# Turning softmax probabilities by four full-array turns a head instead of sixteen quarter-array ones

## The reference

```python
q = (inputs_q @ Wq).reshape(b, sq, H, HD) * (1.0 / np.sqrt(HD))
k = (inputs_kv @ Wk).reshape(b, skv, H, HD)
v = (inputs_kv @ Wv).reshape(b, skv, H, HD)
scores = jnp.einsum('bqhd,bkhd->bhqk', q, k)
attn = jax.nn.softmax(scores, axis=-1)
ctx = jnp.einsum('bhqk,bkhd->bqhd', attn, v).reshape(b, sq, H * HD)
return ctx @ Wo
```

## Time and profile before

| | |
|---|---|
| runs of the kernel before | 1133.2, 1135.2, 1136.26 us |
| median | 1135.2 us |
| profiled execution, from first to last instruction | 1132.8 us |
| TensorE busy in it | 1032.7 us (91%) |
| mean granted TensorE clock in it | 0.950 |
| stage with the change | about 232.5 to 512 us of the span |

### The profile page before, as it was taken

One profiled execution on the slowest core, in us unless ns is written; L12 is line 12 of the kernel. 1 busy time (PEld: TensorE's weight loads), 2 busy tenths in 40 slices (PEclk: granted clock), 3 DMA queues, 4 the chain that ended last, 5 costly groups with the idle time before them and its releaser, 6 DMA issues.

```text
span 1132.8 us, 17516 instructions
## 1 busy us (share of the span) xinstructions
PE 1032.7 (91%) x6658; PEld 691.2 (61%) x6658; DVE 565.9 (50%) x1286; ACT 367.3 (32%) x687; POOL 265.6 (23%) x336
## 2 busy tenths in 40 slices
PE   5979999989999999988865799999959999997989
PEld 4766699446767676757645577777723434453467
DVE  5876423534434343446466221221257787657792
ACT  3562233232121212213311121221204566735660
POOL 5421431500000000003431222222152453302350
PEclk9995999999999999999895999999976999998999
DMA  9003032211011010057017102111010400020000
GB/s 290 25 2 103 19 97 86 84 43 29 22 31 38 25 38 5 11 197 262 1 33 283 33 28 72 69 33 42 14 66 19 157 1 1 2 75 1 0 6 33
DMA packets 37432, 67.25 MB, mean 59 GB/s; under 512 B 4456, under 2 KB 27080, under 8 KB 35816
## 3 DMA queue, kind: packets, MB, share of 16 engines
q1 hardware_dynamic: 29960, 51.98, 13.5%
q0 software_dynamic: 4080, 11.15, 3.5%
q10 hardware_dynamic: 3312, 3.02, 0.8%
HBM read 54.72 MB, written 11.40 MB: 58 GB/s over the span
## 4 chain that ended last, share of the span: by engine, by line
PE 76%; DVE 12%; ACT 5%; DMA 3%; issue 2%; POOL 2%; SPq 0%; DVEq 0%; ACTq 0%; POOLq 0%
PE bank L354 22%; PE bank L1269 12%; PE bank L1293 7%; PE bank L1619 6%; PE bank L2340 5%; PE bank L2365 3%; PE bank L2386 3%; PE bank L1629 3%; PE bank L1282 2%; PE bank L1604 2%; PE bank L2835 2%; PE bank L1594 2%; PE bank L2404 1%; DVE big L2622 1%; DMA big<-yg,big 1%
## 5 line engine op out<-in xcount | busy, mean ns | idle before, releaser
L1269 PE MATMUL bank<-big 128*128 x552 | 147.7, 418 | 0.6 <-ACT big L1154 0.6
L354 PE MATMUL bank<-XNT,big 128*128 128x512 f32 x296 | 137.9, 615 | 7.1 <-DVE big L2575 5.6
L1269 PEld LDWEIGHTS bank<-big 128*128 128x128 f32 x552 | 98.3, 192 | 39.2 <-issue 2.5
L270 POOL TENSOR_TENSOR rstd<-ve,half 128x1 f32<-128x1 f32 x48 | 27.8, 584 | 330.5 <-DVE ve L264 330.2
L2340 PE MATMUL bank<-big,xs 32*128 32x512 f32 x256 | 89.9, 739 | 11.6 <-DVE xs L281 10.1
L354 PEld LDWEIGHTS bank<-XNT,big 128*128 128x128 f32 x296 | 55.8, 196 | 70.8 <-issue 59.9
L2195 DVE TENSOR_REDUCE big<-bank 128x2 f32<-128x512 f32 x128 | 82.0, 685 | 21.1 <-PE bank L2340 20.4
L1293 PE MATMUL bank<-big 128*128 (+1 forms) x368 | 87.2, 380 | 1.1 <-ACT big L1169 1.1
L1047 DVE TENSOR_TENSOR big<-big,bank 128x704 f32<-128x704 f32 x23 | 20.4, 889 | 124.6 <-ACT big L1162 124.6
L2286 ACT ACTIVATE big<-bank 128x1024 f32<-128x1024 f32 x64 | 64.9, 1024 | 40.2 <-PE bank L2365 39.9
L354 PE MATMUL bank<-CTXT,big 128*128 128x512 f32 (+1 forms) x192 | 67.0, 494 | 11.0 <-DMA big<-wvT 11.0
(11 more groups left out here) (350 smaller groups left out, 1803.2 us busy)
## 6 DMA issues: line engine op xcount, KB each, us to landing
big<-m_gu SPq DMA_DIRECT2D x8, 1408.0 KB
big<-m_d SPq DMA_DIRECT2D x8, 768.0 KB
big<-a_qk SPq DMA_DIRECT2D x16, 256.0 KB, 2.9
yg<-big ACTq DMA_DIRECT2D x23, 128.0 KB, 2.1
big<-m_gu SPq DMA_DIRECT2D x8, 352.0 KB
big<-a_o SPq DMA_DIRECT2D x16, 128.0 KB, 2.0
xn<-XNT SPq DMA_DIRECT2D x8, 256.0 KB, 6.0
big<-f_keys SPq DMA_DIRECT2D x1, 2048.0 KB, 9.2
```

The lines of the kernel that those rows point to most:

```text
L270: e.tensor_tensor(k.rstd[at % NT][:, :], k.ve[at % NT][:, :], k.half[:, 0:1], ALU.pow).then_inc(k.ln_rstd, 1)
L354: ins = e.matmul(out, a, b, start=start and n == 0, stop=stop and n == len(pairs) - 1)
L1269: ins = e.matmul(out, xgT[s % 2][:, kb, :], WB[:, bass.ds(at[s] + (kb * 2 * F + c * chunk), chunk)], start=kb == 0, stop=kb == KB - 1)
```

## The change

Two things change, both on TensorE. `turn_p` now issues four turns, each of the full 128 partitions by 128 columns, that is two tiles with both halves. Such a turn moves the block of tile 2i + j and half b to the partitions of half j and the columns of tile 2i + b: half and tile parity change places. So that `pv` still finds each sequence where it looks, `scores` puts another sequence into each block: n = 4(t // 2) + 2b + t % 2 in place of 2t + b. The number and shapes of the matmuls in `scores` stay.

```diff
             for t in range(NT):
                 for b in (0, 1):
-                    c = slice((2 * t + b) * SEQ, (2 * t + b + 1) * SEQ)
+                    n = 4 * (t // 2) + 2 * b + t % 2
+                    c = slice(n * SEQ, (n + 1) * SEQ)
                     ins = e.matmul(bank[b * SEQ:(b + 1) * SEQ, SB_, t * SEQ:(t + 1) * SEQ], qT[h % 2][:, c],
                                    kT[h % FIRST][:, c], start=True, stop=True)
             ins.then_inc(S["s_ps"], 1)
...
             if h > 0:
                 e.wait_ge(S["pt_dve"], h)
-            for t in range(NT):
-                for b in (0, 1):
-                    ins = e.matmul(bank[rows(b), TB, t * SEQ:(t + 1) * SEQ], pb[rows(b), t], k.ident[rows(b), rows(b)],
-                                   start=True, stop=True)
+            for i in range(NT // 2):
+                ins = e.transpose(bank[:, TB, i * P:(i + 1) * P], pb[:, 2 * i:2 * i + 2].rearrange("p t m -> p (t m)"),
+                                  k.ident[:, :])
             ins.then_inc(S["pt_ps"], 1)
```

## The result

| | before | after |
|---|---|---|
| median of the runs | 1134.45 us (4 runs) | 1123.0 us (4 runs, 1122.22 to 1125.54) |
| ratio | | 0.9906, 95% interval 0.9886 to 0.9927 |
| profiled execution, span | 1132.8 us | 1123.8 us (its own time 1125.54) |
| mean granted clock | 0.950 | 0.947 |
| the stage, scores(0) to the start of the last output projection | 269.3 us | 257.9 us |

The changed kernel is faster by 0.7 to 1.1%. The forecast was 1123.3 us. Run again later with six executions, it gave 1122.5 us and a ratio of 0.9907 (0.9885 to 0.9929).

What follows compares the result with a forecast made beforehand. TensorE alone was taken to bound the stage; 0.83 us saved in each of heads 2 to 13, plus heads 0, 1, 14 and 15, made 11.9 us, so 1135.2 - 11.9 = 1123.3 us, range near 1120.3 to 1128.

Steps and rivals of the forecast that it cites:

- What bounds the stage: From 246 to 494 us TensorE alone bounds, busy for 247.76 of 248.00 us, with much room on all other engines.
- The price of the old turn: In a usual head, 1.27 us of TensorE's time: 1.07 for 32 records plus 0.10 lost at each edge.
- the first rival: Turns cost 0.11 us but the edges stay, not made by tiling; 9.4 us saved, 1125.8 us; chance 0.20.
- The price of the new turn: Four full-array turns at 0.11 us each, 0.44 us with no edge cost; a usual head saves 0.83 us.
- The rival of 0.27 each: New turns don't overlap; a usual head saves 0.19 us, 2.3 us in all, 1132.9 us; chance 0.06.
- the slower rival: Turns don't keep the clock up, so it falls mid-stage; 1150 us with one low stretch per head; chance 0.04.
- What is late next: Turned-probabilities copy delays nothing; the output projection's middle pause stays; head 14 loses 0.3 us waiting for ACT's copy.
- The sum: Savings over heads 0 to 15, 11.9 us together, 9.96 of it from heads 2 to 13.
- From the span to the median: Median of the runs taken as 2.4 us above the profiled span, carried over: 1135.2 - 11.9 = 1123.3 us.

Runs made afterwards that it cites:

- quarter pair: Changed kernel with one pair of the old 64 x 64 matmuls added behind the four transposes; 1129.82 us, ratio 0.9966 to the kernel before.
- halves apart: Kernel before with the turn's sixteen 64 x 64 matmuls reordered, eight of the upper half, then eight of the lower; 1147.98 us, ratio 1.0124.
- early projection: In head 15 alone, head 14's output projection goes ahead of the turn; on the changed kernel 1119.25 us (0.9876), on the kernel before 1130.29 us (0.9971).

## Why the prediction was right

- *What bounds the stage.* Right: TensorE alone. What its queue lost, the stage lost; heads 2 to 13 each gave 0.83 or 0.84 us.
- *The price of the old turn, 1.27 us with its edges.* The sum is right, its split is not: 1.08 and 0.10 at each edge is what the starts of the groups show, but 0.14 of the 1.08 are seams as well, so that the sixteen small matmuls are 0.94 and the seams 0.33. Since the new turn removes all of it, the error cancels. The edges vanish with plain full-array matmuls at the same wait, and come back with one quarter pair; in the quarter pair, 0.23 us of its 0.34 are there for the change of tiling, and a short full-array matmul has the rest too. This was the difference between the forecast and the first rival (1125.8), and it is the step that the Trainium skill ("TensorEngine Tiling (Array Packing)", Key Properties) had spoken for; the runs agree that changing the tiling costs time.
- *The price of the new turn, 0.44 us.* Right: 0.437, and 0.109 for each turn added. The rival of 0.27 each took a record's length for its price. The full clock held from 250 to 480 us, so that the slower rival had no case in the usual heads; 0.44 us of turns in 17.68 is all that this shows of it. One argument against that rival was weak: that the clock line shows no low slice around the full-array turns before head 0. A slice of that line is 28 us. The trace before has a stretch of 3.4 us at half clock just behind the second eight of those turns, where TensorE had idle times of 1.46 and 0.78 us too, so that it says nothing on turns either way:

```profile
232.20:235.60 3.40, 3.08 (x4) 1.51 (x5) 0.00 (x0) 0.22 (x1) 0.00 (x0) 0.50 0.00 0
```

- *What is late next.* Right in all three: the copy starts 0.20 us after the projection does, the first addition at 1.14, and head 14 lost 0.3 us to ACT's copy.
- *The sum.* Forecast 11.9 us; the stage gained 11.4. By heads, forecast and measured: head 0 0.45 and 0.50; head 1 0.58 and 0.63; heads 2 to 13 9.96 and 10.03; head 14 0.33 and 0.33; head 15 0.55 and -0.07. The one mis-sized term is head 15, where I let the low stretch end when it did before. It was twice as long and ended 1.4 us later, counted from the turn's start.
- *From the span to the median.* I carried over 2.4 us between them, from three runs of which none is known to be the profiled one; with a fourth run the median before is 1134.45 and not 1135.2, so that the medians are 11.4 us apart where I had said 11.9. In the changed kernel's runs the time is 1.7 us above the span of the same execution. That the median came within 0.3 us is in part luck: an execution's low stretches ahead of and behind the stage alone move it by a few us.

## What to carry to other kernels

In a stage where TensorE is never idle, a matmul costs the distance to the next one's start, and that is read from a row of many; the length of one says nothing. Look at the seams as well: where the block shape changes between neighbours, the price lies in four places (the late start, the first distance inside, the step out, and the first slot behind), and the price of one small matmul must be read from distances between them and not from the group's total. Here it paid to put small matmuls into the shape that stands around them. When a cover gets shorter, ask what it covered, and when TensorE is idle for some us, count the stretch at half clock that may follow as part of the price; filling that hole gave another 3 us here.

## What the runs showed of the hardware

- Float32 turns of 128 x 128 take 0.109 us each when packed, and a plain float32 matmul of the same size 0.22 (two records): a factor of two.
- 64 x 64 matmuls that alternate between two corners of the array take 1.08 us for sixteen; the same ones, one corner after the other, take 1.83. Their records then start one by one, 0.06 us apart; alternating, they start in couples at that distance.
- Going from full-array matmuls to 64 x 64 ones and back costs 0.33 to 0.34 us in all, the same behind plain matmuls (the old turn) as behind transposes (the quarter pair). One full-array matmul of 64 columns in the place of the quarter pair has 0.11 us of this too.
- After 3.86 us without work the clock was at 1.2 GHz for 3.4 us in two profiles with the old turn behind the gap, and for 6.8 us in six with the new turn or a variant of it and in one with the old turn's halves apart. After gaps of only 0.78 and 1.16 us it fell for 3.4 us in both profiles of the changed kernel with the early projection, and didn't in the one of the kernel before with the same edit.
